# A post-norm attention and mixture-of-experts layer on one core: new places for four small steps, and the first loads split by contraction halves

## The reference, cut

```
q = relu(x @ Wq.T + bq) * decay;  k = relu(x @ Wk.T + bk) * decay;  v = x @ Wv.T + bv
kv = einsum("bhnd,bhne->bhde", k, v);  z = 1 / (q . sum_n k + 1e-6)
x1 = layernorm(x + (q @ kv * z) @ Wo.T + bo)
p = softmax(x1 @ w_gate); top 2 of 8, weights normed to sum 1
routed = sum_e combine[t, e] * (silu(g_e) * u_e) @ w_down[e],   g_e, u_e = split(x1 @ w_gate_up[e])
shared = (silu(g) * u) @ w_sh_down,                             g, u = split(x1 @ w_sh_gate_up)
out = layernorm(x1 + routed + shared)
```

## Time and profile before

| | |
|---|---|
| median of three runs | 241.35 us |
| profiled execution: time / span | 242.8 / 241.0 us |
| mean granted TensorE clock | 0.981 of 2.4 GHz |
| TensorE busy (matmul) | 221.6 us, 92% |
| VectorE busy | 154.1 us, 64% |
| ScalarE busy | 115.7 us, 48% |
| GpSimd busy | 137.3 us, 57% |
| HBM read and written | 19.70 and 12.76 MB |

### The profile page before, as it was taken

One profiled execution on the slowest core, in us unless ns is written; L12 is line 12 of the kernel. 1 busy time (PEld: TensorE's weight loads), 2 busy tenths in 40 slices (PEclk: granted clock), 3 DMA queues, 4 the chain that ended last, 5 costly groups with the idle time before them and its releaser, 6 DMA issues.

```text
span 241.0 us, 5038 instructions
## 1 busy us (share of the span) xinstructions
PE 221.6 (92%) x1440; PEld 193.9 (80%) x1440; DVE 154.1 (64%) x528; ACT 115.7 (48%) x298; POOL 137.3 (57%) x163
## 2 busy tenths in 40 slices
PE   8999999989899999979999789999999989999950
PEld 2478888879678888758899679999999978889940
DVE  2762373356767575964889776666666632799960
ACT  2282612761274361257206257778777853413450
POOL 0057689799768877747378006667767772003260
PEclk9999999999999999979999999999999999999995
DMA  6964572422312033002155225656665512961252
GB/s 158 363 218 104 152 252 84 122 62 81 87 47 88 25 110 111 22 33 101 44 184 171 71 84 163 187 171 172 184 175 174 160 53 46 383 196 75 91 176 85
DMA packets 21580, 31.72 MB, mean 132 GB/s; under 512 B 3248, under 2 KB 14257, under 8 KB 21556
## 3 DMA queue, kind: packets, MB, share of 16 engines
q1 hardware_dynamic: 17552, 22.46, 31.3%
q0 software_dynamic: 3456, 8.43, 10.0%
q10 hardware_dynamic: 548, 0.53, 0.8%
HBM read 19.70 MB, written 12.76 MB: 135 GB/s over the span
## 4 chain that ended last, share of the span: by engine, by line
PE 64%; DVE 19%; SPq 4%; issue 4%; ACT 3%; DMA 2%; POOL 1%; POOLq 0%; DVEq 0%
PE bank L335 12%; PE bank L337 12%; PE bank L336 11%; DVE x L1255 4%; PE bank L635 3%; PE bank L377 3%; PE bank L536 3%; PE bank L662 2%; PE bank L561 2%; DVE xt_raw L1064 2%; PE bank L455 2%; SPq L290 2%; PE bank L665 2%; PE bank L653 2%; PE bank L663 2%
## 5 line engine op out<-in xcount | busy, mean ns | idle before, releaser
L1408 POOL DMA_INDIRECT y_pairs<-x_t,dst x40 | 38.9, 973 | 29.5 <-DVE dst L1149 25.3
L1371 POOL DMA_INDIRECT x_slots<-x,slot x32 | 31.9, 996 | 16.5 <-issue 8.3
L335 PE MATMUL bank<-x1t_hi,wf_hi 128*128 128x512 f32 x64 | 26.7, 417 | 1.9 <-DVE xt_raw L1064 1.8
L337 PE MATMUL bank<-x1t_hi,wf_lo 128*128 128x512 f32 x64 | 26.0, 406 | 0.0
L336 PE MATMUL bank<-x1t_lo,wf_hi 128*128 128x512 f32 x64 | 25.8, 403 | 0.0
L335 PE MATMUL bank<-wf_hi,ot_hi 128*128 x80 | 25.7, 322 | 0.0
L1352 POOL TENSOR_TENSOR wf_lo<-stage,wf_hi 128x512 fp32r<-128x512 f32 x18 | 23.2, 1286 | 1.4
L337 PE MATMUL bank<-wf_hi,ot_lo 128*128 x80 | 22.6, 282 | 0.0
L336 PE MATMUL bank<-wf_lo,ot_hi 128*128 x80 | 22.4, 280 | 0.0
L749 ACT ACTIVATE k_sb<-bank,cst 128x256 f32<-128x256 f32 x16 | 7.7, 479 | 30.2 <-PE bank L352 28.5
L1149 DVE SCALAR_TENSOR_TENSOR dst<-o_sb,te_f 128x1 f32 (+1 forms) x40 | 8.8, 220 | 16.6 <-ACT ot_hi L863 16.5
(11 more groups left out here) (181 smaller groups left out, 693.5 us busy)
## 6 DMA issues: line engine op xcount, KB each, us to landing
o_sb<-x_slots SPq DMA_DIRECT2D x40, 129.0 KB
stage<-in_wffn SPq DMA_DIRECT2D x18, 256.0 KB, 2.8
x<-in_x SPq DMA_DIRECT2D x4, 512.0 KB, 7.0
out<-x SPq DMA_DIRECT2D x8, 256.0 KB, 2.1
xt_raw<-in_xT SPq DMA_DIRECT2D x3, 512.0 KB, 6.3
x_slots<-fill SPq DMA_DIRECT2D x9, 129.0 KB, 3.0
x<-in_watt SPq DMA_DIRECT2D x4, 256.0 KB, 6.3
k_sb<-y_pairs SPq DMA_DIRECT2D x2, 512.0 KB, 4.1
```

The lines of the kernel that those rows point to most:

```text
L335: mm(o, w_hi, m_hi, start=start, stop=False, **more)
L337: return mm(o, w_lo, m_hi, start=False, stop=stop, **more)
L1371: pool.indirect_dma_start(out=x_scat, out_offset=bass.IndirectOffsetOnAxis(ap=slot[:, j, t:t + 1], axis=0), in_=x1[:, t, :], in_offset=Non ...
L1408: pool.indirect_dma_start(out=y_scat, out_offset=bass.IndirectOffsetOnAxis(ap=dst[:, j:j + 1], axis=0), in_=ey[:, u, :], in_offset=None, b ...
```

## The change

One edit of loads and four of order; no arithmetic is added or removed.

1. The first loads. Now contraction half 0 of the first x half (128 KB) leads SyncE's queue, followed by weight half 1; weight half 0 leads ScalarE's queue, followed by contraction half 1 of x. `xt_half_in` becomes two semaphores, and TensorE waits for each contraction half apart. ScalarE's first cast needs both.
2. TensorE: `ranks(0)` stands behind `proj_kv(3, 2)` instead of ahead of it.
3. GpSimd: `x1_lo(2)` and then `x1_norm(3)` stand ahead of `scatter(1, 1)` instead of behind it, and in this order.
4. ScalarE and VectorE: `e_silu(0)` and `e_h(0)` stand ahead of `shared_hh(2, 1)` and `shared_lo(2, 1)`.
5. TensorE: chunk (2, 2) of the shared network, which stood behind the experts, is made in two parts of six matmuls in the last two steps of the expert sequence.

```diff
 # SyncE
-            for k in range(KD):
-                w = slice(WKV + k * 2 * D, WKV + (k + 1) * 2 * D)
-                sp.dma_start(wa_raw[:, w], watt[:, w]).then_inc(S["watt_in0" if k == 0 else "watt_in0b"], 16)
+            sp.dma_start(xt_raw[:, 0, 0, 0:SEQ // 2], xT[0][:, 0:SEQ // 2]).then_inc(S["xt_half_in0"], 16)
+            sp.dma_start(wa_raw[:, 2 * D:4 * D], watt[:, 2 * D:4 * D]).then_inc(S["watt_in0b"], 16)
 # TensorE
-                pe.wait_ge(S["xt_half_in"], 16)
                 for k in range(KD):
+                    pe.wait_ge(S[f"xt_half_in{k}"], 16)
                     pe.wait_ge(S["watt_in0" if k == 0 else "watt_in0b"], 16)
...
                     attend(b, range(0, 2))
+                    proj_kv(b + 1, 2)
                     if b >= 2:
                         ranks(b - 2)
-                    proj_kv(b + 1, 2)
                     proj_kv(b + 1, 3)
...
+                if s >= NT - 1:
+                    shared_gu(2, AHEAD, part=s - (NT - 1))
                 if s < NT:
                     e_h_transposed(s, s % RING)
...
-            for c in range(AHEAD, CS):
+            for c in range(AHEAD + 1, CS):
                 shared_gu(2, c)
 # ScalarE
-            load_half(0, S["xt_half_in"])
+            act.dma_start(wa_raw[:, 0:2 * D], watt[:, 0:2 * D]).then_inc(S["watt_in0"], 16)
+            act.dma_start(xt_raw[:, 0, 1, 0:HS], xT[0][:, SEQ:SEQ + HS]).then_inc(S["xt_half_in1"], 16)
...
+            e_silu(0, 0)
             shared_hh(2, 1)
-            e_silu(0, 0)
             e_silu(1, 1)
 # VectorE
+            e_h(0, 0)
             shared_lo(2, 1)
-            e_h(0, 0)
             e_h(1, 1)
 # GpSimd
             scatter(1, 0)
+            x1_lo(NB - 2)
+            x1_norm(3)
             scatter(1, 1)
-            x1_norm(3)
-            x1_lo(NB - 2)
             scatter(2, 0)
```

More of the change, by code:

```diff
@@ L201, in build @@
             watt_in0 watt_in0b watt_in1 watt_in2 kvw_split qw_split ow_split
-            xt_half_in xt_in0 xt_in1 xhi_half_out xlo_half_out xhi_ready xlo_first xlo_ready
+            xt_half_in0 xt_half_in1 xt_in0 xt_in1 xhi_half_out xlo_half_out xhi_ready xlo_first xlo_ready
             res_in0 res_in1 res_in2 res_in3 stage_in0 stage_in1 wf_split fill_made spare_in
@@ L722, in _ @@
             HS = SEQ // 2
-            def load_half(h, into):
-                act.dma_start(xt_raw[:, 0, :, h * HS:(h + 1) * HS],
-                              xT[0].rearrange("p (k n) -> p k n", k=KD)[:, :, h * HS:(h + 1) * HS]).then_inc(into, 16)
-            load_half(0, S["xt_half_in"])
+            act.dma_start(wa_raw[:, 0:2 * D], watt[:, 0:2 * D]).then_inc(S["watt_in0"], 16)
+            act.dma_start(xt_raw[:, 0, 1, 0:HS], xT[0][:, SEQ:SEQ + HS]).then_inc(S["xt_half_in1"], 16)
             act.wait_ge(S["b_cleared"], 2)
@@ L731, in _ @@
             act.dma_start(b_raw[32:33, :], batt).then_inc(S["bias_in"], 16)
-            load_half(1, xt_in[0])
+            act.dma_start(xt_raw[:, 0, :, HS:SEQ], xT[0].rearrange("p (k n) -> p k n", k=KD)[:, :, HS:SEQ]
+                          ).then_inc(xt_in[0], 16)
             activation(warm[:, 1:2], warm[:, 0:1], ACT.Silu)
@@ L802, in shared_hh @@
                 copy(hh(b)[0][:, c, :], hf[:, i % 2, :]).then_inc(S["shh_out"], 1)
-            for h, (loaded, done) in enumerate(((S["xt_half_in"], S["xhi_half_out"]), (xt_in[0], S["xhi_ready"]))):
+            act.wait_ge(S["xt_half_in0"], 16)
+            for h, (loaded, done) in enumerate(((S["xt_half_in1"], S["xhi_half_out"]), (xt_in[0], S["xhi_ready"]))):
                 n = slice(h * SEQ // 2, (h + 1) * SEQ // 2)
```

## The result

The changed kernel takes 239.76 us (median of 16 runs, 239.14 to 244.25) against 242.27 of the kernel before on the same chip (16 runs, 240.14 to 245.03). The ratio is 0.9926, with a 95% interval of 0.9902 to 0.9950: a gain of 1.8 us by the ratio and 2.5 by the medians, less than two per cent. The forecast was 237.1, with a range of 235.9 to 239.2; the time lies 0.56 us above the range. The forecast was taken off a median of three runs, 241.35; over sixteen the kernel before is at 242.27. So of the 2.66 us between 237.1 and 239.76, 0.92 are this base and 1.74 are the gain, 2.51 instead of 4.25.

A forecast was written before the change was run, and what follows sets the result against it. It took TensorE, then VectorE, to bound the kernel, both together in the closing stretch. Terms 0 + 0.65 + 1.95 + 0.95 + 0.35 + 0.35 = 4.25 us off the median 241.35 gave 237.1 us, range 235.9 to 239.2.

The forecast's parts named there:

- Chunk (2, 2): Last expert steps: two matmul groups fill TensorE's waits, shared chunks begin 1.4 us earlier; 0.35 kept, bounds -0.3 and 1.4.
- ranks: TensorE's 1.14 us wait near 62 goes; 0.65 us is kept at x1_transposed(2), bounds 0 and 1.14.
- x1_lo(2), 1.95: Batch 2's top two: VectorE's small operations no longer lengthened by GpSimd's subtraction; 1.95 us, bounds 0 and 2.2.
- clock, 0.95: TensorE's lowered clock at shared_gu(1, 0), costing 1.43 us, recovers with the shorter wait; 0.95 kept, bounds 0 and 1.43.
- Silu and e_h: First expert tile: TensorE's 1.1 us wait before L653 falls to about 0.3; 0.35 us kept, bounds 0 and 1.1.
- Start: First loads: earlier x gains nothing, its second half lands as before; 0 us, bounds -0.25 to +0.7.
- the rival of the late half: First loads: second half of x comes late, 0.35 to 0.7 us lost, 237.45 to 237.8 us; chance 0.10.
- The moved scatters: GpSimd: four scatters behind x1_norm(3) take 5.05 us but cost nothing, covered by batch 3's wait for slots(3).

The follow-up runs named there:

- no_x1lo_c: Changed kernel with GpSimd's x1_lo(2) put back behind scatter(1, 1) and x1_norm(3): 241.78 us, ratio 1.0032 to the kernel before.
- four_groups: Changed kernel with shared chunk (2, 3) also moved ahead of the last down: 241.78 us, ratio 1.0042 to the kernel before.
- no_ranks: Changed kernel with ranks(b - 2) put back ahead of proj_kv(b + 1, 2): 239.15 us, ratio 0.9884 to the kernel before.
- after_c: The changed kernel as it is, run again on a chip like the first: 238.98 us against 241.69 before, ratio 0.9899.

## Why the prediction was wrong, point by point

**Direction and main mechanism** held: a gain of under two per cent, with nearly all of it in x1_lo(2). The size did not: 4.25 forecast, 1.5 to 2.7 measured in three comparisons. The 0.92 us of the base of three runs add to the distance in time, and say nothing of the terms.

**Chunk (2, 2), +0.35 forecast.** This is the step that failed. "The end gains only 210.53 - 210.25" took the send's landing as fixed and pair 1 as the limit. The send was 1.05 us later against the loop, as the 1.35 forecast allowed for, but it lands 1.7 us later on top, and VectorE waits for pair 0; the closing stretch lengthens by 0.66 (45.57 to 46.23). That lies outside the term's bounds of -0.3 and 1.4. TensorE's gain there came (chunk (2, 3) 5.97 earlier, 1.7 more than in the loop, forecast 1.4) and was worth nothing. This term alone is off by 1.0 us, and the time lay 0.56 above the range.

**ranks, 0.65 forecast.** For the execution that was read the term was right: GpSimd's x1_norm(2) would have let `x1_transposed(2)` start 0.7 us earlier. In the first pair it came 1.05 earlier, 0.36 of it because x1_norm(2) ended earlier. But the term took the wait of one execution as the kernel's. It hangs on where GpSimd stands when VectorE reaches three small operations, and is nothing where they miss each other.

**x1_lo(2), 1.95, and clock, 0.95.** Mechanism, places and clock were right. Together they measure 2.3 (forecast 2.9, which is within the interval of 1.2): 1.7 of stall and, by difference, 0.6 of the clock's 1.4. The rest of the clock's gain ends at the first tile, where TensorE stands 1.06 us for a DMA: TensorE was made earlier than the tiles.

**Silu and e_h, 0.35 forecast.** By the traces 0: the 0.35 were there at the second tile and gone at the ninth. The step saw "the next transpose needs e_h_lo(0)", but not the tiles.

**Start, 0 forecast.** The product that needs the second half of x went from 9.99 to 9.70, and lay between 9.36 and 9.89 in the profiles on the two chips like the first. ScalarE's cast of that half began at 9.65 instead of 9.97, so it landed no later and the rival of the late half fell. What the 0.3 are worth at the end was not tried alone, and this edit is the one that no run took back.

**The moved scatters** cost nothing, as forecast: batch 3's wait for slots(3) was 1.11 us instead of 4.17, and its scatters came 4.40 earlier.

**The sum again**, with measured terms: 2.3 + 0 to 0.7 (ranks) - 0.7 and up to 0.3 of the start, 1.6 to 2.6. The three comparisons give 1.8, 2.4 and 1.5 by their ratios. With 1.2 us of uncertainty on the first term alone, their agreement is no proof of the terms. The profiled pair shows 3.6 and so lies near the forecast of 4.25. That is luck of the pair: the profiled execution of before was 0.5 us above its median and had the collision at 62 in full, that of the changed kernel 0.6 below, with a short loop.

## What to carry to other kernels

A small VectorE cast, or a VectorE operation with both inputs in SBUF, ends no sooner than the 128x512 GpSimd operation beside it; one that reads PSUM was not held. Look for VectorE rows that are several times longer than the same form elsewhere, see what GpSimd does there, and move that; one such move was nearly the whole gain of five edits here. A wait that such a collision makes in one execution may be missing in the next, so ask by how much the two engines would have to shift to miss each other before a term is built on it. Fill TensorE's waits ahead of instructions whose result stays on the core, not ahead of the last one of a chain that ends in a transfer another engine waits for.

## What the runs showed of the hardware

An instruction packet of 16 KB takes 0.92 to 1.33 us on its DMA engine near the last send, and the piece of that send that meets it lands 1.10 us behind the packet's end, so a transfer of sixteen pieces and 2.1 us becomes one of 3.7 to 4.3. In the loop, with other transfers about, it was 1.2 us behind the packet in most cases. The Trainium skill (DMA: Bandwidth & Descriptors, Queues, rings and completion order) says that a DMA engine goes from one queue to the next only at packet boundaries; the traces agree in that no such piece landed before the packet's end, and no run shows where the 1.10 us come from.

In the first comparison and on the chips like it the granted clock fell to 0.50 before the last 10 us of the span in four traces of ten, each time 0.9 to 1.5 us after TensorE had stood 1.75 to 1.78 us (before, no_x1lo_c, four_groups, no_ranks). Behind their shorter waits, the longest 1.48 us in after_c, it stayed at 1.00.

Three of the five chips ran this program 9 to 14% longer, with stalls of up to 5.7 us beside GpSimd's rows of scatters. There the same edit was worth 6 us or more that is worth 2.3 on the others.
